# Layer 0's softmax sums in six of eight blocks: the first two groups of heads folded to half the keys by GpSimd, one step of sums on TensorE less

## The reference, cut to what matters

```python
qh = (q @ Wq + bq).reshape(Bn, Tq, H, DK)
attn = jnp.einsum('bqhd,bkhd->hbqk', qh, kh)
attn = attn * mask[None]
attn = attn - jnp.max(attn)
attn = jnp.exp(attn) * mask[None]
attn = attn / (jnp.sum(attn, axis=-1, keepdims=True) + 1e-15)
out = jnp.einsum('hbqk,bkhd->bqhd', attn, vh).reshape(Bn, Tq, H * DK)
out = out @ Wo + bo
```

## Time and profile before

| | before |
|---|---|
| median of 3 runs | 836.01 us (835.39 to 836.18) |
| profiled execution, its own time | 838.48 us |
| its span | 836.5 us |
| TensorE busy | 818.0 us (98%) |
| VectorE / ScalarE / GpSimd busy | 554.9 / 454.9 / 478.5 us |
| mean granted TensorE clock | 0.996 |

### The profile page before, as it was taken

One profiled execution on the slowest core, in us unless ns is written; L12 is line 12 of the kernel. 1 busy time (PEld: TensorE's weight loads), 2 busy tenths in 40 slices (PEclk: granted clock), 3 DMA queues, 4 the chain that ended last, 5 costly groups with the idle time before them and its releaser, 6 DMA issues.

```text
span 836.5 us, 12619 instructions
## 1 busy us (share of the span) xinstructions
PE 818.0 (98%) x4564; PEld 553.5 (66%) x4564; DVE 554.9 (66%) x1278; ACT 454.9 (54%) x575; POOL 478.5 (57%) x311
## 2 busy tenths in 40 slices
PE   8999999999999999998999999999999999999996
PEld 6777475756666575475668677587686775876744
DVE  3568676667676676866764855756648557567577
ACT  4415363736455554726474673864755738647262
POOL 2022404031231403355889989899889898996636
PEclk9999999999999999999999999999999999999999
DMA  9508534251617053799192461562623714612002
GB/s 305 216 24 299 192 131 179 89 217 51 232 42 259 18 203 103 237 334 248 46 220 67 136 193 39 142 174 73 197 72 126 202 38 139 176 51 76 1 26 76
DMA packets 73661, 118.13 MB, mean 141 GB/s; under 512 B 27776, under 2 KB 34176, under 8 KB 73600
## 3 DMA queue, kind: packets, MB, share of 16 engines
q1 hardware_dynamic: 72640, 117.00, 44.6%
q10 hardware_dynamic: 960, 0.34, 0.2%
HBM read 77.47 MB, written 34.08 MB: 133 GB/s over the span
## 4 chain that ended last, share of the span: by engine, by line
PE 83%; DMA 5%; DVE 3%; SPq 3%; issue 2%; POOL 2%; ACT 2%; DVEq 0%; POOLq 0%; ACTq 0%
PE bank L545 19%; PE bank L547 18%; PE bank L546 18%; PE bank L607 6%; PE bank L577 6%; PE bank L584 6%; PE bank L747 3%; PE bank L766 3%; DMA wk_sb<-wk 1%; DMA sums_dram<-sums_out 1%; DVE scores L1397 1%; DMA r_dram<-den 1%; DMA u_dram<-u_out 1%; PE bank L533 1%; DMA r_bc<-r_dram 1%
## 5 line engine op out<-in xcount | busy, mean ns | idle before, releaser
L1639 POOL TENSOR_TENSOR x_lo<-x_raw,x_hi 128x2048 fp32r<-128x2048 f32 (+1 forms) x8 | 35.6, 4450 | 196.5 <-ACT x_hi L930 180.8
L545 PE MATMUL bank<-wo_lo,a_hi 128*128 128x512 f32 x320 | 127.7, 399 | 1.5 <-DVE z L1371 1.5
L546 PE MATMUL bank<-wo_hi,a_lo 128*128 128x512 f32 x320 | 124.7, 390 | 0.0
L547 PE MATMUL bank<-wo_hi,a_hi 128*128 128x512 f32 x320 | 124.7, 390 | 0.0
L1248 DVE CUSTOM_DVE_ANT_0 scores<-bank,mask_f 128x512 f32<-128x512 f32 x128 | 80.9, 687 | 51.9 <-PE bank L577 51.9
L1681 POOL TENSOR_TENSOR a_lo<-a_raw,a_hi 128x1024 fp32r<-128x1024 f32 x32 | 78.0, 2438 | 45.3 <-ACT a_hi L1025 44.5
L545 PE MATMUL bank<-x_lo,wq_hi 128*128 128x512 f32 x256 | 101.2, 395 | 0.6 <-DVE q_lo L1237 0.6
L546 PE MATMUL bank<-x_hi,wq_lo 128*128 128x512 f32 x256 | 99.8, 390 | 0.0
L547 PE MATMUL bank<-x_hi,wq_hi 128*128 128x512 f32 x256 | 99.7, 390 | 0.0
L942 ACT ACTIVATE q_hi<-bank,bq_sb 128x512 fp32r<-128x512 f32 x64 | 44.1, 690 | 101.1 <-PE bank L547 97.9
L1070 ACT ACTIVATE scores<-scores,sh 128x512 f32<-128x512 f32 x128 | 80.2, 711 | 25.1 <-DVE sh L1422 25.0
(11 more groups left out here) (183 smaller groups left out, 1732.7 us busy)
## 6 DMA issues: line engine op xcount, KB each, us to landing
u_dram<-u_out SPq DMA_DIRECT2D x8, 2048.0 KB, 7.6
a_raw<-u_dram SPq DMA_DIRECT2D x32, 512.0 KB, 4.2
r_bc<-r_dram SPq DMA_DIRECT2D x56, 256.0 KB, 5.0
x_raw<-x_t SPq DMA_DIRECT2D x8, 1024.0 KB, 5.6
xn<-x_n SPq DMA_DIRECT2D x8, 1024.0 KB, 5.3
xb_dram<-xn SPq DMA_DIRECT2D x8, 1024.0 KB, 6.0
z<-xb_dram SPq DMA_DIRECT2D x32, 256.0 KB, 2.8
out<-z SPq DMA_DIRECT2D x6, 1024.0 KB, 4.8
```

The costliest lines, as they stand in the source:

```text
L545: nc.tensor.matmul(dst, lh, rl, start=first, stop=False)
L546: nc.tensor.matmul(dst, ll, rh, start=False, stop=False)
L547: return nc.tensor.matmul(dst, lh, rh, start=False, stop=last)
```

## The change: what it does

For blocks 1 to 6 (`FOLDED`) the sums of groups 0 and 1 are prepared by GpSimd. For group 0, the half of `scores` on partitions 64 to 127 is copied by DMA into partitions 0 to 63 of a new buffer `folds`. GpSimd then adds the half on partitions 0 to 63 to it (`fold`). Group 1 is the mirror image: partitions 0 to 63 are copied to 64 to 127 of `folds`. After both folds, `folds` holds the half sums of both groups, one group in each half of the partitions. A new fifth matrix of `summer` sums both in one step of four matmuls (`sums_folded`). So a folded block has three steps of sums: `folds`, group 2, group 3. Group 0 and 1's own steps are left out, and the step on `folds` stands ahead of group 2's.

```diff
+        KEY_HALVES = [slice(0, P // 2), slice(P // 2, P)]
+        FOLDED = range(1, NB - 1)
+        def fold_of(j):
+            return folds[KEY_HALVES[j], :, :]
+        def kept_half(j):
+            return scores[KEY_HALVES[j], HG * j:HG * (j + 1), :]
+        def copied_half(j):
+            return scores[KEY_HALVES[1 - j], HG * j:HG * (j + 1), :]
...
+            def copy_halves(i):
+                if i > FOLDED[0]:
+                    sp.wait_ge(sums_psum_ready, i)
+                for j in range(2):
+                    sp.wait_ge(probs_ready, HG * i + j + 1)
+                    sp.dma_start(fold_of(j), copied_half(j)).then_inc(half_copied[j], 16)
...
                     store_xb(i)
+                    copy_halves(i)
                     load_xn(i + 1)
...
+            def sums_folded(i, dst):
+                pe.wait_ge(folded, fold_count(i, 1))
+                for g in range(G):
+                    nc.tensor.matmul(dst[32 * g:32 * g + 32, :], summer[:, HG, :], folds[:, g, :], start=True, stop=False)
...
-                last = row_sums(SUM_BANK, j)
-                if j == HG - 1:
-                    last.then_inc(sums_psum_ready, 1)
+                if i not in FOLDED or j >= 2:
+                    if i in FOLDED and j == 2:
+                        sums_folded(i, SUM_BANK)
+                    last = row_sums(SUM_BANK, j)
+                    if j == HG - 1:
+                        last.then_inc(sums_psum_ready, 1)
...
+                    save_u(i - 1, 0, 2)
                     x_high(i + 1)
-                    save_u(i - 1)
+                    save_u(i - 1, 2)
...
+                    if i - 1 in FOLDED and h in (0, HG):
+                        dve.wait_ge(folded, fold_count(i - 1, h // HG))
...
+            def fold(i, j):
+                pool.wait_ge(half_copied[j], 16 * (FOLDED.index(i) + 1))
+                if j == 1:
+                    pool.wait_ge(xb_ready, i + 1)
+                nc.gpsimd.tensor_tensor(fold_of(j), fold_of(j), kept_half(j), ALU.add).then_inc(folded, 1)
...
                 x_and_bias(i)
+                if i in FOLDED:
+                    for j in range(2):
+                        fold(i, j)
```

More of the change, by code:

```diff
@@ L84, in named @@
             return (t[name] for name in names.split())
-        put(ctx, "k1_hi k1_lo", [P, C1, B * KEYS], f32r)
+        region(8, lambda k: put(k, "folds", [P, G, QB]), lambda k: put(k, "k1_hi k1_lo", [P, C1, B * KEYS], f32r))
         put(ctx, "v1", [P, B, E1])
-        put(ctx, "summer", [P, HG, 32])
+        put(ctx, "summer", [P, HG + 1, 32])
         put(ctx, "spread_even", [P, QB])
@@ L140, in cross_attention_program @@
         region(2, lambda k: put(k, "bo0_b", [P, D]), lambda k: put(k, "be1_b", [P, D]))
-        k1_hi, k1_lo, v1, ctx_sb, summer, ident = named("k1_hi k1_lo v1 ctx_sb summer ident")
+        folds, k1_hi, k1_lo, v1, ctx_sb, summer, ident = named("folds k1_hi k1_lo v1 ctx_sb summer ident")
         g0_b, bb1_b, g1_b, be1_b, g0_col, bq_sb, bk_sb, bq1_sb = named(
@@ L198, in scaled_count, with fold_count @@
             return (1, 1, 2, 3)[n] if i == 0 else 2 * i + n // 2 + 2
+        KEY_HALVES = [slice(0, P // 2), slice(P // 2, P)]
+        FOLDED = range(1, NB - 1)
+        def fold_count(i, j):
+            return 2 * FOLDED.index(i) + j + 1
+        def fold_of(j):
[4 more added lines that the diff above has]
+            return scores[KEY_HALVES[1 - j], HG * j:HG * (j + 1), :]
         QUADS = [slice(32 * g, 32 * g + 32) for g in range(P // 32)]
@@ L251, in cross_attention_program @@
             "exp_ready probs_ready u_psum_ready sums_psum_ready u_saved")
+        half_copied = [sem(f"half_copied{j}") for j in range(2)]
+        folded = sem("folded")
         m_eps_ready, mhalf_ready, eps_ready, den_ready, rec_ready = sems(
@@ L269, in cross_attention_program @@
             "yt_psum_ready yt_hi_ready yt_ready q1_psum_ready q1_hi_ready q1_ready")
-        logits1_ready, scores1_ready, row1_ready, quad1_ready, top1_ready, base1_ready, shift1_ready, probs1_ready = sems(
-            "logits1_ready scores1_ready row1_ready quad1_ready top1_ready base1_ready shift1_ready probs1_ready")
+        shift_step_ready = sem("shift_step_ready")
+        STEPS = 7
+        logits1_ready, scores1_ready, shift1_ready, probs1_ready = sems(
+            "logits1_ready scores1_ready shift1_ready probs1_ready")
         sums1_psum_ready, turned1_ready, den1_ready, rec1_ready, spread1_ready, u1_psum_ready = sems(
@@ L1403, in head_max @@
                 dve.wait_ge(scores1_ready, H1 * i + MAX_ENDS[g])
-                nc.vector.transpose(key_mx[:], mx1[:]).then_inc(row1_ready, 1)
-                dve.wait_ge(row1_ready, step)
+                before = STEPS * (step - 1)
+                nc.vector.transpose(key_mx[:], mx1[:]).then_inc(shift_step_ready, 1)
+                dve.wait_ge(shift_step_ready, before + 1)
                 for quad, part in enumerate(QUADS):
[L1407 to L1410, removed]
+                    nc.vector.reduce_max(quads[0:32, quad:quad + 1], key_mx[part, :], AX.X).then_inc(shift_step_ready, 1)
+                dve.wait_ge(shift_step_ready, before + 1 + len(QUADS))
+                nc.vector.reduce_max(quad_top[0:32, :], quads[0:32, :], AX.X).then_inc(shift_step_ready, 1)
+                dve.wait_ge(shift_step_ready, before + STEPS - 1)
                 nc.vector.tensor_scalar(head_sh[0:32, :], quad_top[0:32, :], -SCALE1, HEADROOM, ALU.mult,
-                                        ALU.add).then_inc(base1_ready, 1)
+                                        ALU.add).then_inc(shift_step_ready, 1)
             def shift1(i, g):
                 step = N_MAX * i + g + 1
-                dve.wait_ge(base1_ready, step)
+                dve.wait_ge(shift_step_ready, STEPS * step)
                 if i > 0:
@@ L1637, in x_low @@
                 pool.wait_ge(x_hi_ready, i + 1)
+                if i - 2 in FOLDED:
+                    pool.wait_ge(folded, fold_count(i - 2, 1))
                 ks = slice(0, chunks)
@@ L1643, in x_and_bias @@
                 pool.wait_ge(xn_loaded, 16 * (i + 1))
+                if i - 1 in FOLDED:
+                    pool.wait_ge(folded, fold_count(i - 1, 1))
                 if i == NB - 1:
@@ L1852 @@
     mask = np.asarray(mask_BxSxS2_ik1).reshape(NB, QB, KEYS)
-    sum_sel = np.zeros((P, HG, 32), np.float32)
+    sum_sel = np.zeros((P, HG + 1, 32), np.float32)
     for j in range(HG):
         sum_sel[:, j, j] = 1
+    for j in range(2):
+        sum_sel[j * P // 2:(j + 1) * P // 2, HG, j] = 1
     def columns(v, chunks):
```

## The result

The changed kernel takes 847.17 us in the median of four runs (844.18 to 848.75), against 836.1 us before in the same comparison. The ratio is 1.0128, with a 95% interval of 1.0099 to 1.0158: slower by 1.3%, 11 us. The prediction was 842.5 us, in a range of 830 to 850 us. Its profiled execution has a span of 845.3 us.

A forecast was written before the change was run, and what follows sets the result against it. TensorE was taken as the bound, busy 98% of the span and 83% of the chain. Each block saves 0.86 us but waits 1.95: 6 x 1.09 = 6.5 us lost, 836.01 + 6.5 = 842.5 us, range 830 to 850 us.

The forecast's parts named there:

- The step removed, 5.2 us: TensorE, six folded blocks: two steps of sums leave and one comes, saving 0.86 us a block, 5.2 us in all.
- The landing of the copies, 4.4 us: DMA from SBUF to SBUF: each 512 KB copy lands after 4.4 us, copy 0 while the block's third mask runs.
- A fold on 64 partitions costs as much as on 128: GpSimd: a fold of 2048 columns on 64 partitions takes 4.6 us, between bounds of 2.3 and 4.6 us.
- Fold and mask exclude each other: VectorE and GpSimd in SBUF: fold 0 holds the block's fourth mask, which is recorded at about 6.0 us.
- Who goes first when both wait: After fold 0: the fourth mask, issued earlier, goes ahead of fold 1, which runs after it at about 6.7 us.
- The second rival's first form: GpSimd goes from fold 0 straight to fold 1: 5.4 us lost a block, 869 us; chance 0.20 for both forms.
- TensorE's wait, 1.95 us a block: TensorE ahead of the first logits waits 1.95 us for late q_low and saves 0.86: 6.5 us lost in all.
- The second rival's second form (before mask 2), 869 us: Copy lands within 3.4 us, before the third mask; q_low 5 and fourth mask late: 869 us; chance 0.20 for both forms.
- The first rival's condition "after mask 3": Copy lands after more than 6.3 us, in the fourth mask; folds hidden, 5.2 us gained, 830.8 us; rival's chance 0.18.
- The condition "a fold of 2.3 us": Same rival: the fourth mask is held 1.4 us, its slack; 5.2 us gained, 830.8 us; rival's chance 0.18.

The follow-up runs named there:

- experiment 3: Changed kernel with each fold cut to one column of one head, copies and TensorE's three steps kept: 831.54 us, ratio 0.9944 to the kernel before.
- experiment 6: Changed kernel with fold 0 started at the end of mask 1, ahead of mask 2, and copy 0 left out: 864.11 us, ratio 1.0332.
- experiment 1: Changed kernel with both folds held back until mask 3 of the same block has ended, nothing left out: 834.37 us, ratio 0.9976.
- experiment 4: Changed kernel with each fold cut to two of its four heads, 1024 columns in place of 2048: 831.95 us, ratio 0.9945.
- experiment 8: Changed kernel without copies, folds and the step on folds, the rest of the change kept: 836.12 us, ratio 1.0.
- experiment 2: Changed kernel with copies and folds kept, but TensorE doing four steps of sums from scores as before: 843.94 us, ratio 1.008.
- experiment 9: Changed kernel with four more matmuls in each folded block, between the values and the first logits, same output: 845.14 us, ratio 1.0099.
- experiment 10: Changed kernel itself once more, on the chip of experiment 9's run: 848.83 us, ratio 1.0148 to the kernel before.
- experiment 7: Changed kernel with ScalarE's old order, x_hi ahead of all saves, nothing left out: 848.26 us, ratio 1.0138.

## Why the prediction was right, point by point

- **The step removed, 5.2 us**: experiment 3 has 4.3 us in the time and 38.36 instead of 39.2 us a block, 5.0 us in six blocks. Right.
- **The landing of the copies, 4.4 us**: 4.1 to 4.5 us in all twelve. Copy 0 fell inside mask 2, as said. Right, and in part luck: no row showed such a copy, the nearest ones ran from 2.8 to 8.5 us, and a landing 0.9 us earlier would have come ahead of mask 2, as in experiment 6.
- **A fold on 64 partitions costs as much as on 128**: 4.59 us where nothing holds it (experiment 1), against 4.60 us in the earlier trace rows. Right.
- **Fold and mask exclude each other**: mask 3 was to take about 6.0 us; it takes 6.07. Fold 0 and fold 1 were to take 5 to 6 and 6.7 us; they take 5.9 to 6.5 us. Experiments 1, 3 and 4 move or shorten the folds alone, and the loss goes; experiment 8 leaves them out with the copies, and the time is that of before. Shown. It is the Trainium skill's rule ("SBUF — State Buffer", "Who interferes with whom"), and the trace agrees in all six blocks.
- **Who goes first when both wait**: mask 3, although fold 1 is ready (copy 1 has landed some 3 us before). The second rival's first form did not happen.
- **TensorE's wait, 1.95 us a block**: 2.04 us; a block loses 1.24 us net, and I had 1.09.
- **What was off is the size of the sum**: 6.5 us predicted, 11 measured. The term that was missing is the low clock after the wait, 1.6 us in each block where it falls, 3.2 us in the profile after. The prediction does not mention the clock. My sum took TensorE's matmuls at the rows of before, where the granted clock is 1.00 in all of these blocks and TensorE's longest wait is 0.5 us. Experiments 2 and 9, with waits of 1.1 us, have none of it. How often it falls differs from run to run: in the first comparison the changed kernel's fastest run (844.18 us) has a mean clock of 0.994 and its slowest (848.75 us) 0.990. Its runs spread over 4.6 us there and over 7.9 us in the second comparison; not all of that is the clock, since the kernel before spreads over 5.1 us in the second.
- **The range**: 847.17 us lies inside the forecast's 839 to 850 us by luck. The upper bound gave each block 1.2 us more for a late `q_low`. `q_low` was as late as forecast, and the clock used that room.
- **The second rival's second form (before mask 2), 869 us**: experiment 6 has 864 us, with a fold 0 of 3.59 us in place of 4.6 and with the clock at 0.50 in four blocks, which the 869 us did not have. So the mechanism is shown (masks 2 and 3 held, two waits in a block), and the nearness of the two numbers is not.
- **The first rival's condition "after mask 3"**: I gave it the full gain; it has 834.4 us, since head 0 waits for fold 0. Wrong in size. The condition "a fold of 2.3 us" holds: experiment 4 is within 0.5 us of experiment 3.

## What to carry to other kernels

An idle engine is not free work space if it reads the memory of another engine's two-input operations: look at what the other engine does in that very stretch, and how much slack stands behind it. Here 1.6 us of held mask cost nothing and 3.8 us cost 2.0 us of TensorE; cutting the operation so that it held the mask for less than the slack of 1.75 us gave all of the gain. And a wait that appears on an engine that never waited may cost more than its length.

## What the runs showed of the hardware that I had not expected

- TensorE's granted clock fell from 1.00 to 0.50 for 3 to 4 us after waits of 2.04 us, in two of six equal blocks of the changed kernel's profile, one of six in its second (experiment 10) and two of six in experiment 7, and in none of twelve blocks with waits of 1.1 us. What decides between equal blocks stays open. Four more matmuls in each wait made the kernel 3.7 us faster by the medians.
- A GpSimd add of 64 x 2048 took 3.59 us when both inputs were the same rows of `scores`, and 4.59 us with two different ones.
- The trace names ScalarE's save as the releaser of TensorE's wait in the changed kernel, where `q_low` 7 ends 0.1 us after it. Experiments 2 and 9, where a step of sums stands between, name `q_low`, and experiment 7, with the saves later, mostly names none. Where two candidates end that close, the order in the code and one edit decide.
